# Projecting the next batch's k ahead of its q in the last head group of a cross-attention block

## What is computed

```python
q = _layer_norm(query, ln1_g, ln1_b)
qh = (q @ wq + bq).reshape(Bq, Sq, H, hd)
kh = (context @ wk + bk).reshape(Bq, Sc, H, hd)
vh = (context @ wv + bv).reshape(Bq, Sc, H, hd)
scores = jnp.einsum('bqhd,bkhd->bhqk', qh, kh) * scale
scores = jnp.where(allowed[None, None, :, :], scores, NEG_INF)
probs = jax.nn.softmax(scores, axis=-1)
o = jnp.einsum('bhqk,bkhd->bqhd', probs, vh).reshape(Bq, Sq, Dm)
x = query + o @ wo + bo
ff = jax.nn.gelu(_layer_norm(x, ln2_g, ln2_b) @ w1 + b1, approximate=False) @ w2 + b2
return x + ff
```

## Time and profile before

| | us |
|---|---|
| median of 3 runs | 3140.51 (3140.06 to 3140.71) |
| the profiled execution's own time | 3136.32 |
| its span, first to last instruction | 3134.6 |
| TensorE busy in the span | 2976.6 (95%) |
| VectorE busy | 1558.8 (50%) |
| ScalarE busy | 1155.3 (37%) |
| GpSimd busy | 419.7 (13%) |

### The profile page before, as it was taken

How to read it: one execution, slowest core, us unless ns; L and a number is a source line. 1 busy time by engine, 2 the same in 40 slices (tenths; PEclk the granted TensorE clock), 3 DMA queues, 4 the chain that set the end, 5 groups by cost and what they waited for, 6 DMA issues and landing times. The chain is left out here.

```text
span 3134.6 us, 52497 instructions
## 1 busy us (share of the span) xinstructions
PE 2976.6 (95%) x17576; PEld 2409.5 (77%) x17576; DVE 1558.8 (50%) x4164; ACT 1155.3 (37%) x2958; POOL 419.7 (13%) x368
## 2 busy tenths in 40 slices
PE   6999999999999999999969999999999999999999
PEld 5777777777777777777858888888888888888887
DVE  5777667676776767767643432223333222333322
ACT  3655565555655556555532111111111111111111
POOL 1211122111221112211111200000000000000000
PEclk9999999999999999999978999999999999999999
DMA  5765566655666556665533111001111100111100
GB/s 135 117 113 103 104 105 115 110 103 104 105 115 109 103 105 107 113 111 102 91 86 108 41 41 40 9 31 40 40 40 40 40 8 32 40 40 40 40 27 14
DMA packets 123760, 232.42 MB, mean 74 GB/s; under 512 B 10752, under 2 KB 10752, under 8 KB 123648
## 3 DMA queue, kind: packets, MB, share of 16 engines
q1 hardware_dynamic: 123648, 231.28, 36.7%
HBM read 97.02 MB, written 33.55 MB: 42 GB/s over the span
## 5 line engine op out<-in xcount | busy, mean ns | idle before, releaser
L727 ACT ACTIVATE sm<-sm,mins 128x128 f32<-128x128 f32 (+3 forms) x1024 | 571.4, 558 | 645.2 <-DVE mins L581 641.6
L581 DVE CUSTOM_DVE_ANT_0 sm<-bank_s,mask 128x128 f32<-128x128 f32 (+3 forms) x1024 | 479.8, 487 | 454.5 <-PE bank_s L427 444.3
L1159 ACT ACTIVATE g_sb<-bank_f,b1s 128x512 f32<-128x512 f32 x256 | 176.2, 688 | 1173.0 <-PE bank_f L969 1173.0
L1071 DVE CAST g_hi<-g_sb 128x512 fp32r<-128x512 f32 x256 | 112.8, 440 | 867.2 <-ACT g_sb L1159 867.2
L439 PE MATMUL bank_t<-ident,sm 128*128 128x128 f32 x2560 | 427.5, 282 | 52.0 <-DVE pT L522 25.6
L439 PEld LDWEIGHTS bank_t<-ident,sm 128*128 128x128 f32 x2560 | 305.0, 143 | 162.0 <-issue 90.4
L967 PE MATMUL bank_f<-hT_hi,w_hi 128*128 128x512 f32 x1024 | 407.5, 398 | 1.6 <-DVE hT_lo L1065 1.6
L967 PE MATMUL bank_o<-w_hi,g_hi 128*128 128x512 f32 x1024 | 408.0, 398 | 0.0
L969 PE MATMUL bank_f<-hT_hi,w_lo 128*128 128x512 f32 x1024 | 406.7, 397 | 0.0
L968 PE MATMUL bank_f<-hT_lo,w_hi 128*128 128x512 f32 x1024 | 406.4, 397 | 0.0
L969 PE MATMUL bank_o<-w_hi,g_lo 128*128 128x512 f32 x1024 | 406.3, 397 | 0.0
(11 more groups left out here) (108 smaller groups left out, 4378.7 us busy)
## 6 DMA issues: line engine op xcount, KB each, us to landing
stack<-st_hi SPq DMA_DIRECT2D x256, 256.0 KB, 5.7
xt<-in_x SPq DMA_DIRECT2D x32, 1024.0 KB, 5.3
stack<-st_lo SPq DMA_DIRECT2D x128, 256.0 KB, 7.2
c_raw<-in_ctxT SPq DMA_DIRECT2D x64, 256.0 KB, 6.2
x_scratch<-xt SPq DMA_DIRECT2D x64, 256.0 KB, 2.0
xn<-x_scratch SPq DMA_DIRECT2D x16, 1024.0 KB, 7.7
xr<-x_scratch SPq DMA_DIRECT2D x16, 1024.0 KB, 5.6
out<-xr SPq DMA_DIRECT2D x64, 256.0 KB, 2.1
```

The lines of the kernel that those rows point to most:

```text
L581: op = V.tensor_tensor_reduce(sm[:, n % SLOTS_S, off:off + w], bank_s[n % BANKS_S][:, off:off + w], mask[:, 512 - w:512], 1.0, 0.0, ALU.ad ...
L727: op = A.activation(row, row, ACT.Exp, bias=mins[:, g % 2, c:c + 1], scale=-1.0, accum_out=sums[:, g % 2, c:c + 1])
L1071: V.tensor_copy(g_hi[:, f % RING_H, :], g_sb[:, f % 2, :]).then_inc(g_hi_ok, 1)
L1159: A.activation(g_sb[:, f % 2, :], bank_f[f % 2][:], ACT.Gelu, bias=b1s[:, f:f + 1], scale=1.0).then_inc(gelu, 1)
```

## The change

In the last head group `K0` is projected at steps 36 and 37 and `Q0` at steps 38 and 39. A function `turn` swaps 0 and 1 in that group, so that VectorE and SyncE wait for the right count of `qk_hi`, and SyncE issues the copies to `stack` for k ahead of those for q. The other groups, the prologue and `stage_b` are as they were, and the number of instructions of each kind too.

```diff
--- before.py
+++ after.py
@@ -39,6 +39,11 @@
     if k < 4:
         return 0, k, (0, 1)
     return 1, (k - 4) // 2, (2 + (k - 4) % 2,)
+
+
+def turn(w, g):
+
+    return 1 - w if g == HEADS // 4 - 1 else w
 
 
 ACT_MOVES = (5, 9, 11)
@@ -76,7 +81,7 @@
         [("B", {0: 4}), ("Q1", {0: 6, 1: 6}), ("K1", {2: 6, 3: 6}), ("R", {5: 4}), ("V1a", {6: 8, 7: 8, 8: 8}), ("O0", {10: 6, 11: 6})],
         [("Q2", {0: 6, 1: 6}), ("K2", {2: 6, 3: 6}), ("R", {4: 4}), ("O1", {5: 12}), ("O2", {7: 12}), ("O3", {8: 6, 9: 6}), ("V0b", {10: 12, 11: 12})],
         [("Q3", {0: 6, 1: 6}), ("K3", {2: 6, 3: 6}), ("R", {4: 4}), ("V1b", {5: 12, 6: 12}), ("X0", {8: 4}), ("X1", {8: 4}), ("X2", {9: 4}), ("X3", {10: 4})],
-        [("Q0", {0: 6, 1: 6}), ("K0", {2: 6, 3: 6}), ("R", {4: 4}), ("V0a", {6: 8, 7: 4, 8: 4, 9: 4, 10: 4})],
+        [("K0", {0: 6, 1: 6}), ("Q0", {2: 6, 3: 6}), ("R", {4: 4}), ("V0a", {6: 8, 7: 4, 8: 4, 9: 4, 10: 4})],
     ]
     TAIL = [("R", {5: 4}), ("O0", {8: 12}), ("O1", {9: 12}), ("O2", {10: 12}), ("O3", {11: 12})]
 
@@ -267,7 +272,7 @@
                     sp.dma_start(stack[32 * part:32 * part + 32, par, w, :, :].bitcast(F32),
                                  src[:, w, :].bitcast(F32)).then_inc(stacked, 16)
 
-                sp.wait_ge(qk_hi, G * 2 + (w + 1))
+                sp.wait_ge(qk_hi, G * 2 + turn(w, g) + 1)
                 for part in ((0, 1), (0, 2))[w]:
                     copy(part, st_hi)
                 sp.wait_ge(d_free[it.bank(job, g)], it.bank_read(job, g))
@@ -306,7 +311,7 @@
 
                     sp.wait_ge(scored, it.b * TB)
                     sp.sem_inc(carriers, 1)
-                for w, name in enumerate("QK"):
+                for w, name in sorted(enumerate("QK"), key=lambda wn: turn(wn[0], g)):
                     stack_parts(it, w, f"{name}{(g + 1) % NG}", g, (g + 1) % 2, it.b * NG + (g + 1))
 
             def store(it, t):
@@ -562,7 +567,7 @@
             def qk_low(it, job, g, G):
 
                 w, hg, bank = "QK".index(job[0]), int(job[1]), it.bank(job, g)
-                dve.wait_ge(qk_hi, G * 2 + (w + 1))
+                dve.wait_ge(qk_hi, G * 2 + turn(w, g) + 1)
                 bias = bqs[:, hg:hg + 1] if w == 0 else vec[:, 3, hg:hg + 1]
                 V.scalar_tensor_tensor(st_lo[:, w, :], bank_d[bank][:], bias, st_hi[:, w, :].bitcast(F32),
                                        ALU.add, ALU.subtract).then_inc(d_free[bank], 1)
```

## The result

| | before | after |
|---|---|---|
| median, us | 3136.72 (3134.14 to 3140.71, 13 runs) | 3149.23 (3142.56 to 3152.35, 13 runs) |
| the profiled execution, us | 3136.32 | 3152.35 |
| its span, us | 3134.6 | 3150.6 |

The ratio of the times is 1.0037, with a 95% interval of 1.0029 to 1.0044: the change makes the kernel 12.5 us slower.

What follows compares the result with a forecast made beforehand. TensorE was taken to bound the kernel. Fixed waits 14.6, extra clock falls 5.7 and delays in six batches 6.0 made 26.3 us, added to the median 3140.5: 3166.8 us, range 3150 to 3186.

Steps and rivals of the forecast that it cites:

- What bounds the kernel: TensorE bounds `stage_b` and most of `stage_a`; the change matters through its gaps and clock in steps 36 to 39.
- parts 1 to 3: Steps 36 to 39: the 2.05 us idle for x goes; new idles of 0.82 for slice 2, 2.36 for slice 3.
- Part 4, the fixed sum: Step 38 begins its projection 0.97 us later in each full-clock batch, 14.6 us over fifteen.
- the loss is kept: Behind step 38 both orders have the same work and waits, so 0.97 us a batch stays: 14.6 us.
- Part 5, the clock: Clock falls around the gaps of steps 36 to 39: 23.7 after against 18.0 before, plus 6.0 of delays.
- The six delays of 1.0: In six batches with a low clock at step 36's scores, slice 3 comes 1.0 us later: 6.0 us.
- The price before, 18.0: Clock falls in steps 36 to 39 of the kernel before: six batches at 1.94 and four at 1.58 us.
- The single fall, 1.58 us: Steps 36 to 39: one clock fall behind a wait, taken for all fifteen batches after the change, 23.7 us.
- The clock stays up: Rival: two shorter gaps do not bring the clock down; 14.6 - 18.0 = -3.4, 3137 us; chance 0.07.
- The clock falls twice: Rival: each new gap brings the clock down for its own stretch; +53, 3193 us; chance 0.10.
- Slice 3 is there in time: Rival: VectorE reaches the reciprocals 2.36 us earlier, so the wait for slice 3 vanishes; 3102 us; chance 0.03.
- What to look for: Signs: `Q0`'s wait for x gone; fifteen slice waits each of about 0.8 and 2.4, some 48 us in all.

Runs made afterwards that it cites:

- e7: The changed kernel with context slice 3 rounded at the end of step 35 and finished by GpSimd ahead of `expand`: 3107.89 us, 0.9904 of the kernel before.
- e1: The changed kernel without `K0`'s waits for context slices 2 and 3, multiplying slices 0 and 1 twice instead: 3099.42 us, 0.988 of the kernel before.
- e5: The kernel before with 8 useless matmuls ahead of X3's bank wait and 8 ahead of `Q0`'s wait for x: 3118.07 us, 0.9938 of the kernel before.
- e6: The changed kernel with useless matmuls: 8 ahead of X3, 3 and 9 ahead of `K0`'s waits for slices 2 and 3; 3130.63 us.
- e8: e7 with the projections alternating, `K0` at steps 36 and 38, `Q0` at 37 and 39: 3129.01 us, 0.9965 of the kernel before.
- e11: e8 with the next batch's first two context slices loaded behind the `stack` copies of that batch's first head group: 3105.67 us.
- e4: The changed kernel with q's copies to `stack` ahead of k's in the last head group, once both are made: 3240.73 us.
- e12: e4 with the two context loads moved as in e11: 3240.51 us, 1.0328 of the kernel before.

## Why the prediction was right or wrong

**What bounds the kernel, and parts 1 to 3** (the wait for x gone, slices 2 and 3 at 1.57 and 4.63) came out to 0.13 us. That slice 3 stands behind the reciprocals, and these behind the mask of step 37, is shown by e7; that the two new waits are the whole loss, by e1.

**Part 4, the fixed sum.** 0.97 a batch was forecast. It is 0.93 at the end of the four steps in the two kernels as they are (`Q0` at 5.85 against `K0` at 4.92), and 0.97 in the pair without falls. The sentence "the loss is kept" is wrong by a third, as 0.3 us a batch come back at the loop's turn: from the end of the four steps to the next x_low a batch takes 88.52 us in the kernel before and 88.22 in the changed one, 88.54 and 88.20 in e5 and e6. 14.6 should have been about 9.5 to 10. In the two profiles the fourteen batch lengths from the first x_low to the last sum to 10.25 us more.

**Part 5, the clock, is the step that failed.** It was put at 23.7 - 18.0 + 6.0 = +11.7 and is about zero: 20 us before and 19 after (e5, e6). By the lengths of steps 36 to 39 in the two profiles it is 20.8 - 18.0 = +2.8, within the uncertainty of that. Two things were mis-sized in it.
- The six delays of 1.0. Their size was right: in the changed kernel's two batches with a low clock ahead, slice 3 is multiplied from 5.52 and 5.33 on and not from 4.50. But I kept the six batches of the kernel before, as if where the clock falls were a property of the batch. After the change there are two.
- Those two batches have no second fall behind the delay; I had counted both for them. Steps 36 to 39 lost 12 x 1.58 + 1.03 + 0.84 = 20.8 us to the clock and not 29.7.

The price before, 18.0, was right by its own rows. It left out what a fall costs ahead of `Q0`, but the 88.52 and 88.54 us above, with falls and without, show that this is nothing in sum. With +2.8 for the clock, 15 x 0.95 = 14.3 for the steps and 14 x 0.3 = 4.2 back at the turns, the change comes to 12.9 us; 12.5 were measured. So the order of the waits, their lengths and the direction were right by the mechanism forecast, and not by luck; the size was not.

The single fall, 1.58 us, was sized right: the twelve batches end at 10.65 and not 9.07.

**The rivals.** "The clock stays up" did not happen: fourteen batches have a fall. Its number, 3.4 us faster for a clock term of -18, is as far from the measured 12.5 us slower as the forecast; the measured term is about 0. "The clock falls twice" happened in no batch. "Slice 3 is there in time" is what e7 makes of it by an edit, and it gave 3108 where I had worked out 3102. By the Trainium skill (TensorE: Matmul & The Clock Gate, Terms) the penalty is about half of the time at the low clock. That makes 31.8 us in the kernel before (an estimate from its granted clock); filling all gaps gave back 20. The measurement decides: part of the low time lies on waits.

**The median.** I added to 3140.5, the median of three runs. Over 13 runs the kernel before is at 3136.7, and single executions spread by 6 to 10 us. The falls alone do not make this spread: e6, with none between 200 and 1500 us, spreads by 8.5. Its cause is open. Against 3136.7 the range would have begun at 3146 and held the result. Three runs were too few to set the bounds by.

**What to look for** named a wait for slices of 0.8 and 2.4, "some 48 us in all"; the view of waits has 39.9, since it counts a gap from the modelled end of the last matmul. The gaps in the starts are the forecast ones.

## What to carry to other kernels

When work is moved to fill a wait, look up when each of its own inputs is there, down to the slice, and in which in-order streams they stand; here the moved work's last input was 2.4 us late, and moving that input too turned a loss of 12 us into a gain of 30. Do not carry the clock's falls batch by batch from one order to another: price them as a whole, by filling the gaps in both kernels. And when a copy is said to be "hidden by so many steps", subtract its issue and its landing from those steps; what was left of eight steps here was under three microseconds. And keep large loads off the DMA queues where the loop turns: with two of them moved e8 became some 20 us faster (e11).

## What the runs showed of the hardware

- At a turn of the batch loop VectorE's first instruction starts 1.6 to 2.0 us behind two 8 KB packets of the "instruction" DMA queue. Where two loads of 256 KB, issued 9 to 10 us ahead, are still moving then, these packets come behind them, and the instruction starts 3.7 us behind the scores that it needs; with the loads moved away it is 2.2 (e8 and e4 against e11 and e12); elsewhere in a batch it is 0.7.
- In e1 TensorE's clock goes to 1.2 GHz behind a gap of 2.0 us in fourteen of fifteen batches. Which gaps do it differs from batch to batch with the same work, so equal batches of the kernel before took from 96.6 to 98.6 us. In the changed kernel the fall sat at the same place in twelve batches in a row, and these took 98.8 to 99.1.
- Six transfers of 256 KB issued within 4 us on one queue land up to 10.7 us behind their issue (e4), against 6.6 at most where they come by threes (the changed kernel, batch at 709.1).
- Rounding a 128x512 tile on VectorE takes 1.11 us and not 0.41 while GpSimd subtracts a tile (e7), and ends 0.29 behind it.
